# Two graph layers on one core: layer 2 with adjacency as the weights, fewer score tiles on VectorE, V loaded by two queues, and the last group's weights added in pairs

## What is computed

```python
h = max(layernorm(x), 0)
scores = (h @ W @ a1)[:, None] + (V @ W @ a2)[None, :]
e = where(scores > 0, scores, 0.2 * scores)
e = where(adj > 0, e, -9e15)
x = x + elu(softmax(e, axis=1) @ V + h)
h2 = max(layernorm(x), 0)
deg = adj.sum(axis=0)
x = x + max((adj.T @ h2) @ U.T / deg[:, None], 0)
```

## Time and profile before

| | us |
|---|---|
| median of 3 runs | 490.03 |
| the profiled execution | 489.36 |
| its span, first to last instruction | 487.5 |
| TensorE busy | 425.2 (87%) |
| VectorE busy | 299.1 (61%) |
| ScalarE busy | 255.0 (52%) |
| POOL busy | 127.8 (26%) |

### The profile page before, as it was taken

The page is one execution under the profiler, slowest core; times in us unless marked ns, Lnnn a source line. Parts: engine busy times, 40 slices in busy tenths (PEclk is TensorE's granted clock), DMA queues, the critical chain, the costliest instruction groups (busy, mean ns, idle before and its releaser), DMA issues.

```text
span 487.5 us, 9207 instructions
## 1 busy us (share of the span) xinstructions
PE 425.2 (87%) x3966; PEld 200.5 (41%) x3966; DVE 299.1 (61%) x401; ACT 255.0 (52%) x306; POOL 127.8 (26%) x118
## 2 busy tenths in 40 slices
PE   0511989799987999998999999999999999999996
PEld 0411344354332544332444333354333436655563
DVE  4799489669999578999469999523443313101011
ACT  1210457575654776776776766877777741100010
POOL 8750058476242702321202223101010001200000
PEclk9975699799999999999999999999999999999999
DMA  9799999999999790000000000000000000000001
GB/s 162 83 107 108 107 102 107 108 107 109 107 102 101 77 99 1 1 2 0 1 1 2 1 1 1 1 1 1 1 1 2 1 1 3 0 12 12 21 19 27
DMA packets 17638, 20.74 MB, mean 43 GB/s; under 512 B 13409, under 2 KB 13473, under 8 KB 17598
## 3 DMA queue, kind: packets, MB, share of 16 engines
q0 software_dynamic: 4752, 16.90, 33.5%
q1 hardware_dynamic: 8606, 2.18, 2.3%
q10 hardware_dynamic: 4240, 1.08, 1.3%
HBM read 69.79 MB, written 1.05 MB: 145 GB/s over the span
## 4 chain that ended last, share of the span: by engine, by line
PE 60%; DVE 23%; issue 9%; ACT 4%; DMA 2%; ACTq 1%; POOL 1%; DVEq 0%; POOLq 0%
PE att L988 16%; DVE junk L692 14%; PE q L972 10%; PE den L991 9%; PE q L1077 7%; DVE arena L738 5%; PE q L1047 3%; PE den L1077 3%; DMA v_sb<-n_L_gnn_entity_embs_dram 2%; PE att L1077 2%; PE z L937 2%; ACT q L529 2%; PE z L952 2%; ACT arena L513 2%; PE z L1093 1%
## 5 line engine op out<-in xcount | busy, mean ns | idle before, releaser
L988 PE MATMUL att<-arena,v_sb 128*64 128x500 f32 (+2 forms) x640 | 151.1, 541 | 5.0 <-ACT arena L517 3.2
L692 DVE CUSTOM_DVE_ANT_0 junk<-adj_sb,t_row 125x2048 uint8<-125x2048 uint8 x66 | 153.5, 2326 | 0.7
L738 DVE SCALAR_TENSOR_TENSOR arena<-arena,b_col,q 128x1000 f32<-128x1000 f32 (+2 forms) x80 | 85.7, 1071 | 89.5 <-PE q L972 89.5
L517 ACT ACTIVATE arena<-arena,t 128x1000 f32<-128x1000 f32 (+2 forms) x80 | 78.6, 982 | 89.0 <-DVE arena L738 88.9
L972 PE MATMUL q<-bi,adj_sb 128*128 128x125 bf16 (+1 forms) x1088 | 90.1, 221 | 14.7 <-ACT q L529 9.8
L991 PE MATMUL den<-arena,ones 128*32 128x250 f32 (+1 forms) x1280 | 94.5, 354 | 0.0
L972 PEld LDWEIGHTS q<-bi,adj_sb 128*128 128x128 fp8e4 x1088 | 64.4, 99 | 72.1 <-issue 42.9
L529 ACT ACTIVATE q<-arena,minus_b 128x1000 f32<-128x1000 f32 (+2 forms) x80 | 76.0, 950 | 7.3 <-PE q L963 1.2
L513 ACT ACTIVATE arena<-q,t_col 128x1000 f32<-128x1000 f32 (+2 forms) x80 | 74.7, 934 | 2.8 <-PE q L972 2.4
L991 PEld LDWEIGHTS den<-arena,ones 128*32 128x32 f32 x1280 | 25.4, 109 | 107.9 <-issue 107.9
L988 PEld LDWEIGHTS att<-arena,v_sb 128*64 128x64 f32 x640 | 32.2, 137 | 22.8 <-ACT arena L517 5.6
(11 more groups left out here) (152 smaller groups left out, 295.6 us busy)
## 6 DMA issues: line engine op xcount, KB each, us to landing
adj_sb<-in_adj_dram POOLq DMA_DIRECT2D x33, 500.0 KB, 28.6
v_sb<-n_L_gnn_entity_embs_dram ACTq DMA_DIRECT2D x4, 256.0 KB, 9.1
x_sb<-in_x_dram SPq DMA_DIRECT2D x1, 928.0 KB
out_dram<-x_sb SPq DMA_DIRECT2D x7, 124.0 KB
x_sb<-in_x_dram SPq DMA_DIRECT2D x1, 125.0 KB
out_dram<-x_sb SPq DMA_DIRECT2D x1, 125.0 KB
buf_a<-in_L_gnn_a_dram ACTq DMA_DIRECT2D x1, 32.0 KB, 3.0
buf_b<-in_L_gnn_U_dram SPq DMA_DIRECT2D x2, 16.0 KB, 6.4
```

The source lines that it names most:

```text
L517: nc.scalar.activation(e_part(n % E_SLOTS, nb), e_part(n % E_SLOTS, nb), ACT.Exp, bias=t02[:, c:c + 1])\
L692: nc.vector.tensor_tensor_reduce(out=junk[0:R, :], in0=adj_bytes[0:R, b, half], in1=t_row[0:R, half], scale=1.0 / ONE, scalar=0.0, op0=ALU ...
L738: nc.vector.scalar_tensor_tensor(out=e_part(n % E_SLOTS, nb), in0=a_part(nb), scalar=b_col[:, c:c + 1], in1=part(q[0], nb), op0=ALU.max, o ...
L988: nc.tensor.matmul(att[h * D:(h + 1) * D, 0:(k1 - k0) * R], v_sb[:, c, :], e[:, k0 * R:k1 * R], start=first, stop=final)
```

## The change

- **Layer 2 turned round.** The adjacency block is the weight (124 or 125 columns of fp8), and 129 columns of `h2` pass: the high half, the low half and a column of ones whose sum is the degree. The results come in natural form, up to three blocks to a bank, in 12 OUTS over eight banks. `count`, `degrees`, `product` and their copies are gone. U is applied before: h2 of each group is turned (`turn_h2`, c = 17), copied by ScalarE (18), multiplied by U (`times_u`, 19) and split (20). Rows of U are scaled to norm 1 first (VectorE, and a power on POOL ahead of `power(1)`), and VectorE multiplies the norm back in at the end. Each block of outputs takes five VectorE steps and two stores (112 rows, then the rest). The gathers of outs 0 to 5 over blocks 0 to 24 go ahead of the last group's close, whose blocks follow.
- **Leaky parts shared per group.** ON_DVE = (12, 6, 12, 12, 16) tiles of each group go by VectorE, spread evenly; the rest by ScalarE. Both kinds use q[n % 2], and ScalarE's relu of a tile waits for the exp of the tile two before. The product that seeded q[1] (L963) is gone.
- **V by two queues.** ScalarE issues chunks 0 and 2, SP chunks 1 and 3 ahead of x. POOL sets five constant rows instead of nine before its part of V, and doesn't wait for x before the adjacency loads.
- **The V average** (`mean_v`) goes from tiles 2 to 5 of group 0 to a place before the first shifts; shifts are turned in bf16; `to_natural` uses true transposes.
- **Pairs in the last group.** VectorE adds the e of two tiles (`pair`), and TensorE multiplies with ones once for both (`weigh_pair`). e has seven slots there, four of them in `t_row`.

```diff
@@ constants
-    ONES_FIRST = 9
+    ONES_FIRST = 5
-    ON_ACT = [c % 2 == 1 for i, c in TILES]
+    ON_DVE = (12, 6, 12, 12, 16)
+    ON_ACT = [c >= 2 and (c - 1) * (ON_DVE[i] - 2) // (NC - 2) == (c - 2) * (ON_DVE[i] - 2) // (NC - 2) for i, c in TILES]
+    LAST = NI - 1
+    LAST_SLOTS, PAIRS = 7, NC // 2
-    CHUNKS = [(4 * i, 4 * i + 4) for i in range(7)] + [(28, 29), (29, 33)]
+    OUTS = [(3 * i, 3 * i + 3) for i in range(9)] + [(27, 29), (29, 31), (31, 33)]
+    PART_A = 6
+    STORE = 112
@@ sync
             sp.dma_start(w_sb, W[:, :]).then_inc(wa_in, 16)
+            load_v(1)
+            load_v(3)
             sp.dma_start(x_sb[:, 0:SHORT, :], x_short).then_inc(x_in, 16)
...
+                sp.dma_start(to[0:STORE], x_sb[0:STORE, b0:b1, :]).then_inc(out_stored, 16)
+                sp.dma_start(to[STORE:rows], x_sb[STORE:rows, b0:b1, :]).then_inc(out_stored, 16)
@@ gpsimd
-            pool.wait_ge(x_in, 32)
             for b in range(ONES_FIRST):
                 load(b)
+            for b in range(ONES_FIRST, 7):
+                set_ones(b)
+                load(b)
...
+            pool.wait_ge(u_bounded, 1)
+            pool.wait_ge(ones_made, 1)
+            nc.gpsimd.tensor_tensor(u_inverse[:, :], u_squares[:, :], minus_half[0:D, 0:1], ALU.pow).then_inc(u_inverted, 1)
             power(1)
@@ scalar
-            for i in range(PARTS):
+            for i in (0, 2):
...
+            def copy_turned(i):
...
+                act.wait_ge(h2_turned, i + 1)
...
+                nc.scalar.activation(h_t[:, 0:both], z[:, 0, 0:both], ACT.Copy).then_inc(h2_turned_copied, 1)
             def high(i):
...
-                act.wait_ge(h2_done, i + 1)
-                nc.scalar.activation(h2[0:R, b0:b1, 0:D], buf_a[0:R, 0:b1 - b0, :], ACT.Copy).then_inc(hi_done, 1)
+                act.wait_ge(h2_multiplied, i + 1)
+                nc.scalar.activation(h2[0:R, b0:b1, 0:D], product, ACT.Copy).then_inc(hi_done, 1)
+                nc.scalar.activation(buf_a[0:R, 0:b1 - b0, :], product, ACT.Copy).then_inc(h2_copied, 1)
...
-                nc.scalar.activation(part(q[1], nb), a_part(nb), ACT.Relu, bias=minus_b[:, c:c + 1]).then_inc(relued, 1)
+                act.wait_ge(exped, n - Q_SLOTS + 1)
+                nc.scalar.activation(part(q[n % Q_SLOTS], nb), a_part(nb), ACT.Relu, bias=minus_b[:, c:c + 1]).then_inc(relued, 1)
@@ vector
+            def pair(m):
+                n = NC * LAST + 2 * m
...
+                dve.wait_ge(exped, n + 2)
+                dve.wait_ge(weighed, n + 1)
+                nc.vector.tensor_tensor(e_slot(n, nb), e_slot(n, nb), e_slot(n + 1, nb), ALU.add).then_inc(paired, 1)
...
+                nc.vector.reciprocal(rdeg[0:rows, 0:nb].unsqueeze(2), sums(o)[:, :, 2 * D:2 * D + 1]).then_inc(rdeg_done, 1)
+                nc.vector.tensor_reduce(mine, sums(o)[:, :, 0:2 * D].rearrange("p k (h d) -> p k d h", h=2), AX.X, ALU.add)\
...
+                nc.vector.scalar_tensor_tensor(out=mine, in0=mine, scalar=0.0, in1=rdeg[0:rows, 0:nb].unsqueeze(2).to_broadcast([rows, nb, D]),
...
+                nc.vector.tensor_tensor(mine, mine, u_scale[0:rows, :].unsqueeze(1).to_broadcast([rows, nb, D]), ALU.mult)\
...
+                nc.vector.tensor_tensor(x_sb[0:rows, b0:b1, :], x_sb[0:rows, b0:b1, :], mine, ALU.add).then_inc(fin_done, 1)
@@ tensor
+            def weigh_pair(m):
...
+                pe.wait_ge(paired, m + 1)
+                for k, (k0, count) in enumerate(quarters(nb)):
+                    last = nc.tensor.matmul(den[32 * k:32 * k + 32, 0:count * R], ones32[:, :], e[:, k0 * R:(k0 + count) * R],
+                                            start=(m == 0), stop=(m == PAIRS - 1))
+                last.then_inc(pair_weighed, 1)
...
+                if i == LAST and c >= 5 and c % 2 == 1:
+                    weigh_pair((c - 5) // 2)
+                if i >= 1 and c == TURN_H2:
+                    turn_h2(i - 1)
+                if i >= 1 and c == TIMES_U:
+                    times_u(i - 1)
...
+            def gather(o, first, last_one):
...
+                if o >= 8:
+                    pe.wait_ge(fin_done, o - 7)
+                for k in range(b1 - b0):
+                    start = first_row(b0 + k)
+                    for b in range(first, last_one):
+                        rows = rows_of(b)
+                        done = nc.tensor.matmul(out_bank(o)[0:out_rows, k * (2 * D + 1):(k + 1) * (2 * D + 1)],
+                                                adj_sb[0:rows, b, start:start + out_rows], h2[0:rows, b, 0:2 * D + 1],
+                                                start=(b == 0 and k == 0), stop=(b == NB - 1 and k == b1 - b0 - 1))
...
+            late = GROUPS[-1][0]
...
+            gather(0, 0, late)
             to_natural(NI - 1)
+            for o in (1, 2, 3):
+                gather(o, 0, late)
+            turn_h2(NI - 1)
+            gather(4, 0, late)
+            times_u(NI - 1)
+            gather(5, 0, late)
+            pe.wait_ge(lo_done, NI)
+            for o in range(PART_A):
+                gather(o, late, NB)
+            for o in range(PART_A, len(OUTS)):
+                gather(o, 0, NB)
```

More of the change, by code:

```diff
@@ L820, in _ @@
                     scores(n, GROUPS[i][1] - GROUPS[i][0], i, c)
+                if i == LAST and c >= 3 and c % 2 == 1:
+                    pair((c - 3) // 2)
                 if i >= 1:
@@ L987, in attend @@
                 for h, (k0, k1) in enumerate(((0, half), (half, nb))):
[L988 to L989 removed]
+                    last = nc.tensor.matmul(att[h * D:(h + 1) * D, 0:(k1 - k0) * R], v_sb[:, c, :], e[:, k0 * R:k1 * R],
+                                            start=first, stop=final)
+                if i == LAST:
+                    last.then_inc(weighed, 1)
+                    return
                 for k, (k0, count) in enumerate(quarters(nb)):
```

341 lines of the change are left out of this document (173 added, 168 removed).

## The result

The changed kernel takes 477.84 us (median of 4 runs, 474.8 to 479.38) against 489.76 for the kernel before (4 runs): a ratio of 0.976, 95% interval 0.973 to 0.979. It is 12 us faster where 48 were forecast, and outside the range of 433 to 470. The profiled execution took 476.75 us with a span of 474.9.

What follows compares the result with a forecast made beforehand. TensorE was taken to bound groups 2 and 3, the last group and layer 2, but not groups 0 and 1. Stages 42.7 + 51 + 61.3 + 148.5 + 67.2 + 69 = 439.7, plus 2.53, gave 442.2 us; range 433 to 470.

Steps and rivals of the forecast that it cites:

- The start: Before group 0: V loads on two queues make t ready near 13.2 us; 46.7 becomes 42.7 us.
- Group 0: First attention group: fewer scores and other moved work take it from 59.2 to 51 us, bounds 47 and 57.
- The last group: Final attention group: halved weighings by ones take it from 74.3 to 67.2 us, bounds 65.5 and 71.
- the term of 9.0 us: Last group, TensorE: 16 of 32 weighings by ones go, at 0.56 us each.
- The cover: Last group: ScalarE's 3.3 us and VectorE's 2.5 per pair fit under TensorE's 3.68, with 0.8 us of stall.
- Layer 2: Adjacency as weights: 1089 pairs at 56.3 ns, 61.3 us, loads hidden; 88.8 becomes 69 us.
- Both rivals on the loads: Layer 2: loads bind at 103 ns a pair, 493 us (12 in 100); loads half hidden, about 80 ns, 468 us (8).
- Group 1: Second attention group: fewer scores among VectorE's guards take it from 66.0 to 61.3 us, bounds 59.5 and 66.
- groups 2 and 3: Fewer VectorE scores ahead of tile 26 recover 4 of TensorE's 6.9 us idling; 152.5 becomes 148.5 us.
- a late one holds masks and weighings; I count 0.5 us a group in the bounds: Groups 2 and 3: h2's turn at tile 17 or product with U at 19, if late, stalls TensorE.
- the account: Groups 0 and 1: sum of VectorE's guards, scores and other work plus six tiles; gave 66.1 against 66.0 measured for group 1.
- the attention doesn't follow: Rival, attention groups: queued scores, relus, turn and product wait; groups 0 to 3 give half, 454 us; 15 in 100.

Runs made afterwards that it cites:

- the block kernel: Changed kernel with sum_s behind tile 24, tiles in strict turn, except even tiles 8 to 16 of groups 0 to 3 also ScalarE's: 452.30 us.
- the later sum_s and strict turns: Changed kernel with sum_s behind tile 24 instead of 21 and tiles alternating strictly (VectorE even, ScalarE odd from 3): 459.46 us.
- the run without pairs: Kernel with sum_s behind tile 24 and strictly alternating tiles, the last group's products with ones made per tile again: 464.02 us against 459.46.
- cause A: Late h2 chain making VectorE wait at sum_s; tested by moving sum_s from tile 21 to 24 in the changed kernel: 463.10 us.
- cause C: Copy of rows waiting for VectorE's score of tile 31; tested by exchanging engines of tiles 30 and 31 in the changed kernel: 470.69 us.
- The relief itself: Tiles 8 to 16 of groups 0 to 3 all ScalarE's: kernel before 484.06 us; changed kernel with sum_s behind 24, otherwise strictly alternating tiles, 452.30 us.
- cause D: Tile 1's score behind a guard; moving it and copies of den and att earlier, with sum_s behind 24 and tiles 30, 31 exchanged: 450.13 us.
- later + exchanged: Changed kernel with sum_s behind tile 24 and the engines of tiles 30 and 31 exchanged in every group: 452.74 us.
- all that helped: Changed kernel, sum_s behind 24, group-start score and copies ahead of guard, groups 0 to 3 alternating with tiles 8 to 16 ScalarE's: 448.21 us.
- the earlier chain: Changed kernel, sum_s still behind tile 21, h2's turn and copy behind tile 16, product with U and high half behind 18: 471.62 us.

## Why the prediction was wrong, step by step

- **The start** (42.7, 42.1) was right: t is ready at 13.15 us, and VectorE does not wait for x. **Group 0** (51, 52.65) is within its bounds; the block kernel, 47.1 from its first mask and some 48 from where the stage begins, comes near the low bound of 47.
- **The last group** (67.2, 68.7) is within its bounds, in part by where it is cut: by the old boundaries it is some 70.6. The work was right. In the kernel with the later sum_s and strict turns, whose boundaries are the old ones, TensorE is busy 66.42 us where 66.4 were computed, so the term of 9.0 us stands against the kernel before (0.56 for a set ahead of a mask; behind another set, as in the run without pairs, it is less). The cover was not: there TensorE idles 3.75 us, not 0.8, and in the changed kernel all its waits in this group are for ScalarE, which was one of the prediction's signs of being wrong. The turn was covered as computed, with 2.7 us to spare.
- **Layer 2** (69, 69.8) was right, and with it the choice on which the forecast hung: the load is hidden. The pair was 2.1 ns too cheap, 2.3 us in all, and the tail 1.4 us shorter than estimated. Both rivals on the loads fall. Of the sign of being wrong, rows of 130 ns or more and pairs over 60 ns, the first half came (135 ns) and not the second, so a row's length was no sign. The rows agree with the rule cited from the Trainium skill, TensorE: Matmul & The Clock Gate, Weight-path perf modes, by which the fast load wants exactly 128 weights: 98 ns against 135. Of the 103 ns that the same page's section LDWEIGHTS gives for 124 columns (an estimate by its columns / 1.2) and the 81 ns of its section Back-to-back issue gap for sustained pairs the trace bears out neither: the pace is 58.4 ns whether the load's row shows 135 ns or 98.
- **Group 1** (61.3, 67.35) and **groups 2 and 3** (148.5, 174.3) were wrong. The step that failed is "a late one holds masks and weighings; I count 0.5 us a group in the bounds". It followed the moved steps on TensorE's queue and stopped there. The high half moved from tile 17 to tile 20 on ScalarE; behind it come the low half and weigh_h on GpSimd, and behind these sum_s, in order on VectorE at tile 21, with guards and scores behind it. Nothing was missing for that: the step numbers stand in the kernel and in the change. In place of 0.5 us a group the runs showed cause A at 14.7 us in all (moving sum_s alone), of which 9.2 are waits of TensorE and the rest its lower clock.
- **The share-out** was priced as a count of scores only. Which tile changes hands was not looked at: tile 31 (cause C, 7.1 us alone, 10.4 on top of A's cure) and tile 1 (cause D, 2.6). The relief itself came at about half its price, 5.2 us in the kernel before and 7.2 in the changed one against the 11 to 14 that I drew from the account for that run, and nearly all ahead of group 2; the 4 us in groups 2 and 3 are 0.7 at most.
- **The rival "the attention doesn't follow"** named scores behind guards, relus in order, and turn and product waiting, and that is what happened, but for the turn and the product: no wait ahead of them stands among TensorE's. Its price was half of the gain and 3 more, 454 us (its 16.7 should read 16.9, which moves it by 0.1). It let a gain vanish and not turn into a loss: 23 us more than before in three groups, where a lower clock follows some of the longer stalls. TensorE's busy time in group 2 is 77.35 us with the stalls and 72.39 without the longest of them (later + exchanged), for the same work but three instructions.

With all that helped the kernel takes 448.2 us, 6 over the forecast; its share-out in groups 0 to 3 is no longer the change's. In its profiled execution, whose span is 9.6 over the sum of the stages, groups 2 and 3 hold 5.9 of that and the last group 2.2. What is still open: how much of A is the wait and how much is the place. The one run on it gives 6.2 us to the earlier chain, which leaves 8.5 for the rest, but the earlier chain also made ScalarE wait 4.0 us for the product with U. And why a pair takes 58.4 ns and not 56.3 was not tried.

## What to carry to other kernels

Where a step is moved in one engine's order, follow what it releases through every engine until the chain comes back to the bound one, and note at which tile that is: here one copy that stood three tiles later met a reduction of 0.7 us without slack, and 14.7 of the 48 us forecast were lost at it. When work is shared out anew, look at the tiles at a group's edges (the first two and the last), since single buffers and drains hang on them, and expect a gain only in stages where the bound engine idles. With the later sum_s and strict turns TensorE was busy 85 and 90% of groups 0 and 1 and 94 and 93% of groups 2 and 3. VectorE's own share did not tell: 82% in group 0, where relief gave 6.2 us, and 84% in group 2, where it gave nothing. When a large change gives little, compare stage by stage first: one view showed that four stages had come out near their forecast and two rows had turned. And cut the stages at the same place in every engine's order, or a boundary that moved looks like a gain.
